# Mixer of a two-half megakernel: products of two units in one run of TensorE, four decay buffers, near decays by absolute value

## What is computed

```
xn    = layer norm of x (as the program fuses it), then per token:
proj  = xn @ in_proj_w.T          # gate 4096, x 4096, B 8*128, C 8*128, dt 64
xBC   = silu(causal conv of 4 taps over x, B, C)
dt    = softplus(dt + dt_bias);  dA = exp(-dt * exp(A_log))
state = state * dA + (dt * x) (outer) B         # for each of 64 heads, along the sequence
y     = state . C + D * x
y     = group rms norm(y) * norm_weight * silu(gate)
s     = y @ out_proj_w.T
out   : four-stream mixing of xn with 50 Sinkhorn iterations, a branch product, SiLU, times s, plus x
```

## Time and profile before

| | us |
|---|---|
| median of 3 runs (lowest, highest) | 3055.89 (3054.63, 3057.09) |
| the profiled execution, its own time | 3054.47 |
| its span | 3053.0 |
| TensorE busy | 3000.2 (98%) |
| weight loads busy | 2341.8 (77%) |
| VectorE busy | 2128.1 (70%) |
| ScalarE busy | 1763.6 (58%) |
| GpSimd busy | 687.7 (23%) |

### The profile page before, as it was taken

How to read it: one execution, slowest core, us unless ns; L and a number is a source line. 1 busy time by engine, 2 the same in 40 slices (tenths; PEclk the granted TensorE clock), 3 DMA queues, 4 the chain that set the end, 5 groups by cost and what they waited for, 6 DMA issues and landing times.

```text
span 3053.0 us, 45217 instructions
## 1 busy us (share of the span) xinstructions
PE 3000.2 (98%) x14352; PEld 2341.8 (77%) x14352; DVE 2128.1 (70%) x2648; ACT 1763.6 (58%) x3728; POOL 687.7 (23%) x575
## 2 busy tenths in 40 slices
PE   8999999999999998999999999999999999999998
PEld 7777777777777777777777777777777788887787
DVE  7667667576666685767666666766667878677877
ACT  5667575757666575576665757575665332234443
POOL 4222213121222134413222231212124000001112
PEclk9999999999999999999999999999999999999999
DMA  3534343443434353435243433434254444456665
GB/s 138 169 126 158 108 159 107 141 138 110 155 110 155 114 197 98 157 121 172 95 168 104 157 123 135 139 109 160 90 171 153 148 138 150 146 196 211 209 212 182
DMA packets 125532, 444.90 MB, mean 146 GB/s; under 512 B 17488, under 2 KB 21712, under 8 KB 109008
## 3 DMA queue, kind: packets, MB, share of 16 engines
q1 hardware_dynamic: 117552, 423.14, 41.1%
q0 software_dynamic: 4096, 14.68, 1.2%
q10 hardware_dynamic: 3744, 5.51, 0.6%
HBM read 397.86 MB, written 45.42 MB: 145 GB/s over the span
## 4 chain that ended last, share of the span: by engine, by line
PE 82%; issue 5%; DVE 4%; POOL 2%; ACT 2%; DMA 2%; DVEq 0%; SPq 0%; ACTq 0%; POOLq 0%
PE bank L1101 18%; PE bank L1103 17%; PE bank L1102 17%; PE bank L1139 9%; PE bank L1361 5%; PE bank L1362 5%; PE bank L1363 5%; PE bank L1113 2%; PE bank L1125 2%; DMA acc<-in_w_out 1%; PE bank L1149 1%; POOL gate L467 1%; DVE acc L839 1%; DVE x_lo L1356 1%; DVE x_lo L1355 1%
## 5 line engine op out<-in xcount | busy, mean ns | idle before, releaser
L1101 PE MATMUL bank<-x_hi,w_hi 128*128 128x512 f32 x2576 | 1024.6, 398 | 2.4 <-DVE acc L839 2.4
L1103 PE MATMUL bank<-x_hi,w_lo 128*128 128x512 f32 x2576 | 1003.0, 389 | 0.0
L1102 PE MATMUL bank<-x_lo,w_hi 128*128 128x512 f32 x2576 | 1000.9, 389 | 0.0
L839 DVE SCALAR_TENSOR_TENSOR acc<-bank,conv_w,acc 128x511 f32<-128x511 f32 (+2 forms) x576 | 430.8, 748 | 270.5 <-ACT acc L616 241.9
L1101 PEld LDWEIGHTS bank<-x_hi,w_hi 128*128 128x128 f32 x2576 | 484.1, 188 | 114.7 <-issue 22.2
L1103 PEld LDWEIGHTS bank<-x_hi,w_lo 128*128 128x128 f32 x2576 | 484.0, 188 | 102.6
L1102 PEld LDWEIGHTS bank<-x_lo,w_hi 128*128 128x128 f32 x2576 | 484.9, 188 | 93.6
L616 ACT ACTIVATE acc<-bank,tap_par 128x512 f32<-128x512 f32 x192 | 149.5, 779 | 517.0 <-PE bank L1103 486.0
L1361 PE MATMUL bank<-x_hi 128*128 128x512 f32 x1008 | 394.7, 392 | 8.9 <-DVE x_lo L1356 5.3
L1362 PE MATMUL bank<-x_lo,x_hi 128*128 128x512 f32 x1008 | 393.1, 390 | 0.0
L1363 PE MATMUL bank<-x_hi,x_lo 128*128 128x512 f32 x1008 | 392.9, 390 | 0.0
(11 more groups left out here) (165 smaller groups left out, 3408.0 us busy)
## 6 DMA issues: line engine op xcount, KB each, us to landing
units<-cum_scratch SPq DMA_DIRECT2D x128, 1280.0 KB, 6.7
w_raw<-in_w_in SPq DMA_DIRECT2D x160, 512.0 KB, 3.7
w_raw<-y_scratch SPq DMA_DIRECT2D x128, 512.0 KB, 3.6
y_scratch<-gate SPq DMA_DIRECT2D x32, 1024.0 KB, 6.5
acc<-in_w_out SPq DMA_DIRECT2D x128, 256.0 KB, 3.8
xbc<-in_x SPq DMA_DIRECT2D x16, 512.0 KB, 5.6
units<-in_x SPq DMA_DIRECT2D x16, 512.0 KB, 3.7
rstd_b<-rc_scratch SPq DMA_DIRECT2D x32, 256.0 KB, 4.3
```

The costliest lines, as they stand in the source:

```text
L839: dve.scalar_tensor_tensor(acc[:, s % 2, back:], bank_proj[s % 2][:, 0:SEQ - back], mix.conv_w[:, at, m, 3 - back:4 - back], acc[:, s % 2, ...
L1101: pe.matmul(out, w_hi[m % 2][:, k, :], hi, start=(k == 0), stop=False)
L1102: pe.matmul(out, w_hi[m % 2][:, k, :], lo, start=False, stop=False)
L1103: mm = pe.matmul(out, w_lo[m % 2][:, k, :], hi, start=False, stop=(k == KT - 1))
```

## The change

It has six parts. (1) `RING` 3 to 4: a fourth decay buffer. (2) The plans: products of two units stand in one slot, turns too, with slots for exponentials, weighing and turns written out; `turn_x` uses two banks, 2 and 7 (7 is also a bank of the scores), sums, `rc`, `rb`, `scale` and stores of both sequences move. (3) To make room in memory: `w_raw` and `th` with one buffer instead of two, the mask with 256 columns instead of 512 (what lies beyond is copied, not multiplied), the output's raw tiles in `xbc`. (4) Near decays: Abs with the negated running sum `falls` as bias instead of Relu with `cum`; far exponentials with the same bias and scale -1 instead of `dec`, and rows of the table stored accordingly (`far` with six tables in three dependent steps). (5) At slot 12 the last tanh and SiLU stand first. (6) Order of the last pieces among the output's first products, slots of the output's first loads, `load_small` behind unit 6.

```diff
-RING = 3
+RING = 4
-        self.w_raw = sb("w_raw", [P, 2, KT, P])
+        self.w_raw = sb("w_raw", [P, KT, P])
-        self.acc, self.th = sb("acc", [P, 2, SEQ]), sb("th", [P, 2, SEQ])
+        self.acc, self.th = sb("acc", [P, 2, SEQ]), sb("th", [P, SEQ])
-        self.cum = sb("cum", [P, NT, HEADS])
-        self.dec = sb("dec", [P, NT, HEADS])
+        self.falls = sb("falls", [P, NT, HEADS])
...
-        self.exp = exp or [s - 3 + h for s in mult for h in range(2)]
-        self.turn = [s - 2 for s in mult]
-        self.attn = [s - 1 for s in mult]
+        self.load, self.exp, self.attn, self.turn, self.mult = load, exp, attn, turn, mult
         self.square = [s + 1 for s in mult]
         self.gate = [max(s + 1, gate_from + 1 + u) for u, s in enumerate(mult)]
-        self.norm = [s + 2 for s in mult[-SEQS:]]
-        self.var = [s + 3 for s in mult[-SEQS:]]
-        self.rc = [s + 4 for s in mult[-SEQS:]]
-        self.rb = [s + 5 for s in mult[-SEQS:]]
-        self.scale = [s + 6 for s in mult[-SEQS:]]
-        self.store = [s + 7 for s in mult[-SEQS:]]
+        self.norm = [s + norm_after for s in mult[-SEQS:]]
+        self.var = [s + 1 for s in self.norm]
+        self.rc = [s + 3 for s in self.norm]
+        self.rb = [s + 3 for s in self.norm]
+        self.scale = [s + 4 for s in self.norm]
+        self.store = [s + 5 + q for q, s in enumerate(self.norm)]
...
-FIRST = Plan(cb=[9, 11], load=[9, 10, 12, 14, 15, 17, 19, 20], mult=[13, 14, 16, 18, 19, 21, 23, 24],
-LATER = Plan(cb=[5, 7], load=[4, 5, 7, 10, 12, 14, 16, 18], mult=[9, 11, 13, 15, 17, 19, 21, 23],
-LAST = Plan(cb=[5, 7], load=[4, 5, 7, 10, 12, 14, 15, 17], mult=[9, 11, 13, 14, 16, 18, 20, 21],
-            gate_from=CONV_SLOTS, exp=[6, 7, 8, 9, 10, 11, 11, 12, 13, 14, 15, 16, 17, 18, 18, 19])
+FIRST = Plan(cb=[9, 11], load=[9, 10, 12, 13, 16, 17, 19, 20],
+             exp=[10, 11, 12, 13, 13, 14, 15, 16, 17, 17, 18, 18, 20, 20, 21, 21],
+             attn=[12, 14, 16, 17, 19, 20, 22, 23], turn=[13, 13, 15, 15, 18, 18, 20, 20],
+             mult=[15, 15, 18, 18, 20, 20, 23, 23], gate_from=CONV_SLOTS, norm_after=3)
+LATER = Plan(cb=[4, 6], load=[5, 6, 9, 10, 13, 14, 17, 18],
+             exp=[6, 7, 8, 9, 10, 11, 12, 13, 14, 15, 16, 17, 18, 19, 20, 21],
+             attn=[8, 10, 12, 14, 16, 18, 20, 22], turn=[8, 8, 11, 11, 15, 15, 19, 19],
+             mult=[11, 11, 15, 15, 19, 19, 23, 23], gate_from=CONV_SLOTS, norm_after=3)
+LAST = Plan(cb=[4, 6], load=[5, 6, 8, 9, 12, 13, 15, 16],
+            exp=[6, 7, 8, 9, 9, 10, 11, 12, 13, 13, 14, 15, 16, 16, 17, 18],
+            attn=[8, 10, 11, 13, 15, 16, 18, 19], turn=[8, 8, 11, 11, 14, 14, 17, 17],
+            mult=[11, 11, 14, 14, 17, 17, 20, 20], gate_from=CONV_SLOTS, norm_after=2)
+OUTPUT_LOADS = [SLOTS - 5, SLOTS - 4]
...
-    bank_tr = core.bank[2]
+    bank_tr = [core.bank[2], core.bank[7]]
...
         def load_w(g, at, m):
             n = TILES * g + m
-            need(sp, w_split, n - 1)
-            sp.dma_start(w_raw[:, m % 2, :, :], w_tiles[TILES * at + ORDER[m]]).then_inc(w_loaded[m % 2], 16)
+            need(sp, w_split, n)
+            sp.dma_start(w_raw[:, :, :], w_tiles[TILES * at + ORDER[m]]).then_inc(w_loaded, 16)
...
-            need(sp, multiplied, UNITS * (half * GROUPS - 1) + UNITS - 2)
+            need(sp, multiplied, UNITS * (half * GROUPS - 1) + UNITS - 1)
             sp.dma_start(small_raw, d["w_small"]).then_inc(early_of[half].small_loaded, 16)
...
-                    ahead = s // 2 + 3
+                    ahead = s // 2 + 2
...
         def tanh(g, s):
             act.wait_ge(conv_taken, CONV_SLOTS * g + s + 1)
-            act.activation(th[:, s % 2, :], acc[:, s % 2, :], ACT.Tanh).then_inc(tanh_done, 1)
+            if s:
+                act.wait_ge(silu_done, CONV_SLOTS * g + s)
+            else:
+                need(act, gate_done, GATE_SLOTS * g)
+            act.activation(th[:, :], acc[:, s % 2, :], ACT.Tanh).then_inc(tanh_done, 1)
...
-                op = act.activation(part, part, ACT.Relu, bias=mix.cum[:, CHUNKS * q + k, head], scale=-1.0)
+                op = act.activation(part, part, ACT.Abs, bias=mix.falls[:, CHUNKS * q + k, head], scale=-1.0)
...
-                act.activation(part, part, ACT.Exp, bias=mix.dec[:, CHUNKS * q + k, head])
+                act.activation(part, part, ACT.Exp, bias=mix.falls[:, CHUNKS * q + k, head], scale=-1.0)
...
-                op = dve.tensor_tensor(bc[:, q, OFFSET[k]:OFFSET[k] + WIDTH[k]], cb_out[k],
-                                       core.mask[:, 0:WIDTH[k]], ALU.mult)
+                near = min(WIDTH[k], 2 * P)
+                if WIDTH[k] > near:
+                    dve.tensor_copy(bc[:, q, OFFSET[k] + near:OFFSET[k] + WIDTH[k]], cb_out[k][:, near:])
+                op = dve.tensor_tensor(bc[:, q, OFFSET[k]:OFFSET[k] + near], cb_out[k][:, 0:near],
+                                       core.mask[:, 0:near], ALU.mult)
...
             c, q = divmod(u, SEQS)
             pe.wait_ge(silu_done, CONV_SLOTS * g + 2 * SEQS + u + 1)
-            need(pe, dtx_done, UNITS * g + u)
+            need(pe, dtx_done, UNITS * g + u - 1)
+            if u == 1:
+                pe.wait_ge(bc_done, SEQS * (g + 1))
...
-        drain(piece, HALVES - 1, SLOTS, LAST.mult[-1])
+        pe.wait_ge(dtx_done, UNITS * HALVES * GROUPS)
         pe.wait_ge(bc_done, SEQS * HALVES * GROUPS)
         pe.wait_ge(gate_taken, GATE_SLOTS * HALVES * GROUPS)
         first_products(0, (3, 4, 7, 0, 1))
-        drain(piece, HALVES - 1, LAST.mult[-1], LAST.norm[0])
+        drain(piece, HALVES - 1, SLOTS, LAST.norm[0])
         first_products(1, (3, 4, 7, 0, 1))
-        drain(piece, HALVES - 1, LAST.norm[0], LAST.norm[1])
         pe.wait_ge(y_done, UNITS * HALVES * GROUPS)
         for j in range(2):
             first_products(j, (5, 6))
-        drain(piece, HALVES - 1, LAST.norm[1])
+        drain(piece, HALVES - 1, LAST.norm[0])
```

More of the change, by code:

```diff
@@ L175 @@
 SCALE_AT = [{t: [0, 1] if t == 0 else [t + 1] for t in range(NT - 1)}, {2: [4], 3: [5], 4: [6], 6: [7]}]
-RSTD_AT = [{t: [t] for t in range(NT)}, {1: [4], 3: [5], 4: [6], 6: [7]}]
+RSTD_AT = [{t: [t] for t in range(NT)}, {1: [4], 2: [5, 6], 5: [7]}]
 AHEAD_LOAD = [8, 8, 12, 15, 19]
@@ L255, in mixer_programs @@
     w_branch = sq[:, :].rearrange("p (k c) -> p k c", c=CW)
-    far = sums[:, 0, 0:3 * SEQS * HEADS].rearrange("p (a q h) -> p a q h", a=3, q=SEQS)
-    cum_hm = bc[0:HEADS, :, :]
-    causal, ones, one = core.mask[:, 0:P], core.mask[:, P:2 * P], core.mask[:, SEQ - 1:SEQ]
+    far = flat(sums)[:, 0:6 * SEQS * HEADS].rearrange("p (q a h) -> p q a h", a=6, q=SEQS)
+    rows_hm = bc[0:HEADS, :, :]
+    causal, ones, one = core.mask[:, 0:P], core.mask[:, P:2 * P], core.mask[:, 2 * P - 1:2 * P]
     d_heads = rstd_b[:, 1, 0:HEADS]
@@ L402, in step @@
                         load_w(g + 1, after(at, plan), ahead - TILES)
-                    elif ahead < TILES + 2:
-                        sp.wait_ge(w_split, TILES * g + ahead - 1)
-                        sp.wait_ge(silu_done, CONV_SLOTS * (g + 1))
-                        output.load(sp, 0, 0, ahead - TILES)
+                if ends_all(half, plan) and s in OUTPUT_LOADS:
+                    sp.wait_ge(cb_done, SEQS * (g + 1))
+                    sp.wait_ge(silu_done, CONV_SLOTS * (g + 1))
+                    output.load(sp, 0, 0, OUTPUT_LOADS.index(s))
                 for group in open_groups(g, s, half, plan, before):
@@ L1034, in early @@
                 dve.wait_ge(e.cum_copied, 1)
-                dve.tensor_tensor(far[:, 0], cum[:, :, 2, :], tot[:, :, 1, :], ALU.add).then_inc(e.far_step, 1)
-                dve.tensor_tensor(far[:, 1], cum[:, :, 3, :], tot[:, :, 2, :], ALU.add).then_inc(e.far_step, 1)
-                dve.wait_ge(e.far_step, 2)
-                dve.tensor_tensor(far[:, 2], far[:, 1], tot[:, :, 1, :], ALU.add).then_inc(e.far_step, 1)
-                dve.tensor_tensor(mix.dec[:, :, :], by_head(bank_tot[:, :]), mix.cum[:, :, :],
-                                  ALU.subtract).then_inc(e.far_step, 1)
+                for n in range(3):
+                    at = (0, 3, 5)[n]
+                    last = falls[:, :, 1:, :] if n == 0 else far[:, :, at - 3 + n:at, :]
+                    if n:
+                        dve.wait_ge(e.far_step, n)
+                    dve.tensor_tensor(far[:, :, at:at + 3 - n, :], last, tot[:, :, 0:3 - n, :],
+                                      ALU.subtract).then_inc(e.far_step, 1)
             t = s - 2
@@ L1248, in turn_cum @@
             need(pe, e.cum_hm_copied, 3 * q)
-            near = [mix.cum[:, CHUNKS * q + k, :] for k in range(CHUNKS)]
-            ahead = [far[:, a, q, :] for a in range(3)]
-            for i, table in enumerate([near[0], near[1], ahead[0], ahead[2], near[1], near[2], ahead[1],
-                                       near[2], near[3], near[3]]):
+            near = [mix.falls[:, CHUNKS * q + k, :] for k in range(CHUNKS)]
```

(3 more changed lines are left out.)

60 lines of the change are left out of this document (29 added, 31 removed).

## The result

The changed kernel takes 3084.79 us, the median of 5 runs (3082.01 to 3087.98), against 3056.06 of 5 runs of the kernel before: a ratio of 1.0092, 95% interval 1.0081 to 1.0103. It is slower by 28.7; 3061 was forecast, at most 3076.

The account below looks back on a forecast made before the run. TensorE was taken to set the time. Inner groups -15.6, FIRST +22.4, LAST -1.0, between halves -4.3 and end +3.3 sum to +4.8: 3059.3 for the profiled execution, 3061 as median; range 3040 to 3076.

Parts of the forecast that it names:

- Inner groups, -1.3 each: Six inner groups a half: fewer runs, shape changes and turns save 1.9, two returning waits leave -1.3 each, -15.6 for twelve.
- The wait of turn 1: Inner groups: turn 1 shares bank 7 with the scores and waits for both masks, 0.3.
- that of `project(10)`: Inner groups: `project(10)` waits for its bank until VectorE's conv, behind `split_lo` and `weigh`, is done, 0.3.
- FIRST, +11.2 for the group: FIRST, one group a half: six fewer runs -1.5, but late ScalarE and VectorE work makes products wait; +11.2 (8 to 15) each.
- 1.0 for the clock: FIRST: TensorE, idle while waiting, loses its clock and runs at 1.2 GHz instead of 2.4; 1.0 (0 to 3).
- LAST, -0.5 each: LAST groups, one a half: turns merged and one run fewer, -0.5 each, -1.0 in all.
- the cover of the single `w_raw`: Load goes out two slots ahead (11 us, needs 4); costed at nothing; if cover goes, each late microsecond is paid per tile.
- Between the halves, -4.3: From turn 7 to the transposes behind the second small product: 30.0 before, now shorter by 4.3 (-6 to -1).
- End of the mixer, +3.3: Last gate frees bank 1 late, so output products start later: +2.6 and 0.7 for the clock, +3.3 (0 to 5).
- The late store of the gate (b): Slower rival: second half of `gate` stored in slot 12 lands late, 14 groups pay 1.1: +15, 3076; chance 0.14.
- That of the clock (c): Slower rival: waits in FIRST and at the end leave 1.2 GHz stretches, 1.7 each: +6, 3066; part of a 0.2 chance.
- FIRST without its waits (a): Faster rival: ScalarE not so late in slot 1 behind FIRST; FIRST gives -1, total -19.6, 3036; chance 0.27.

Follow-up runs that it names:

- four small moves: Changed kernel, pairs kept: FIRST's squares 4, 5 and last head to slot 22; LAST's unit 4 load to slot 11, squares 4, 5 to 19: 3060.22, single execution.
- the run with the moved issue: Changed kernel with the load of unit 4's decays in slot 12 of LAST issued ahead of load_w instead of behind it: 3083.31, single execution.

## Why the prediction was wrong

**Inner groups, -1.3 each: right.** Ten of them gained 1.5 each (137.8 to 138.3 for the forecast 138.2). The wait of turn 1 did not come, that of `project(10)` did (0.2 in its row), and in some groups 0.2 before a gate.

**FIRST, +11.2 for the group, 9.9 with the inner group's own gain taken off: right in size.** Measured +10.5 and +11.4. Product 6 waits 6.3 where 6.2 stood in the sum, product 5 waits 2.6 where 1.3 stood, product 7 only 1.0 where 3.7 stood: while TensorE is late for product 6, VectorE goes on with the next conv and weighing. The half speed behind the wait took up the difference: from product 6 to product 7 it took 5.56, of which 1.03 waited, so product 6 itself took 2.2 more than the 2.30 of a plain one, where I had 1.0 for the clock. The weighing of unit 6 ended 22.9 behind the run in slot 20, for 22.7 in the sum. The microsecond lost to GpSimd fell on it (3.88), and only 0.3 on the low part, where I had put all of it.

**LAST, -0.5 each: this is the step that failed.** It stood in one sentence: "Turns merged, one run fewer". I had worked FIRST through from engine to engine and costed the other packed plan by TensorE's stream alone, as if ScalarE and VectorE were as far ahead as in LATER. Measured +11.9 and +6.9 up to slot 19, which is 19.8 of the 28.7 by which the sum fell short of the profiled execution. What the runs show in its place: with the slots of before the loss is gone (e.g. 170.46 for 170.44), four slots in place of three for units 2 and 3 take it away up to slot 19, the statistics make 5.3 of it in half 0, and the load behind `load_w` makes 4 in half 0; these overlap and do not add up. What was wrong is the overlap: ScalarE and VectorE were taken to be ready in LAST, and they are not with two units in three slots. I had even written that the cover of the single `w_raw` might go and what each late microsecond would then cost, and had looked for it behind FIRST alone.

**Between the halves, -4.3: measured -1.4.** From the end of slot 19 (1173.88) to the transposes behind the second small product (1202.33) it takes 28.5, where 25.7 was forecast. The order was right. The clock was not:

```profile
1162.00:1200.00 38.00, 31.17 (x165) 25.20 (x166) 24.90 (x37) 22.49 (x41) 24.64 (x27) 0.82 0.25 80
```

In 38 us 0.82 is granted. The first small product takes 5.03 where the second takes 2.88, and the products of each set of sums lie 1.51 apart from first to last instead of 0.70. I had 0.7 for it. Over the stage itself, 1173.9 to 1202.4, 0.76 is granted; before, from 1158.0 to 1188.1, it was 0.89.

**End of the mixer, +3.3: measured +8.8 to the end of the program, of which 1.1 lies behind the output's 91st product.** TensorE waits 6.6 where 5 was forecast, which is ScalarE's squares: the second starts 4.2 behind the first, not 2.73, because GpSimd's add between them took 2.90 instead of 1.3. The rest is the clock again (15 output products in 6.3 instead of 3.5) and a low part 1.7 late behind it.

**The rivals.** The late store of the gate (b) did not hold TensorE: no inner group is over 138.3. Its wait does exist in LAST. ScalarE stands 2.2 before the gate of slot 13 in half 0 and 3.6 in half 1, until 1126.87 and 2301.53; the stores issued at 1119.83 and 2293.15 had landed 7.0 and 8.3 later, 0.1 before. In both halves the decays came later still, so it cost nothing of its own. That of the clock (c) gave the right direction and less than it cost. FIRST without its waits (a) was wrong. None of them had the packing of LAST in it, so the range could not hold the result, 3084.8.

## What to carry to other kernels

A schedule written by hand has as many budgets as plans. Where an edit packs the same work into fewer slots, every engine's load per slot must be added up in every plan, and most carefully in the shortest one; the gain of the long plan says nothing of it. Here the pairs are worth 15 us where they have four slots each. Where two units had three slots or fewer the new plans cost 48, and the run with pairs in LATER only gets that back; with four small moves about half of it comes back although the pairs stay (3060.22).

Taking one wait away from a chain in which two engines are full moves the wait to the next link: three of the single moves ended in another wait. A cheap test is to give one stage its old plan back, and to read the stage and not the sum.

A buffer saved makes the wait on its load longer, and in a queue that issues in the program's order everything behind that load waits too, also what has nothing to do with the buffer.

## What the runs showed of the hardware

**A wait costs more than its length.** Behind the waits of 4.3 and over the products ran slow: the stretches behind two of them in LAST (the first rows are the wait, the second what followed):

```profile
1136.30:1141.50 5.20, 0.17 (x1) 0.00 (x0) 1.21 (x2) 5.20 (x14) 0.00 (x0) 0.71 0.01 4
1141.50:1147.50 6.00, 5.93 (x18) 4.80 (x19) 5.97 (x10) 6.00 (x18) 1.34 (x1) 0.68 0.83 256
...
2309.80:2314.40 4.60, 0.34 (x2) 0.00 (x0) 1.23 (x2) 4.60 (x13) 0.00 (x0) 0.81 0.00 0
2314.40:2328.00 13.60, 13.54 (x50) 11.02 (x51) 8.72 (x9) 12.13 (x30) 4.38 (x3) 0.81 0.89 332
```

The two slots at 2314.45 took 13.37 instead of 11.0, so 2.4 on top of a wait of 4.3; those at 1141.57 12.78, 1.8 on top of 5.1; the output products 2.7 on top of 6.6. The waits of 2.1 and 1.5 before slots 13 and 14 were followed by 24 products at the plain pitch. Between these the length alone does not decide: a wait of 2.6 (187.12 above) was followed by a product at the plain length of 2.38, one of 2.4 in the run with the moved issue by a product of 4.07. The Trainium skill ("TensorE: Matmul & The Clock Gate", section "What's actually happening") calls the throttled clock the default, released by activity. These rows agree in kind: behind the waits the products first start 0.43 apart and then 0.23, so the 0.68 and 0.81 are mixtures of half speed (1.2 GHz) and full speed (2.4 GHz). I had put at most 1.7 on such a wait.

**GpSimd and VectorE hold each other up both ways.** The timelines of VectorE and GpSimd at the end of the mixer:

```profile
2344.93 2.83 DVE L887 TENSOR_TENSOR units<-units,bc 128x2560 f32<-128x2560 f32 x1 [1.15 <-ACT units L665]
```
```profile
2345.98 2.90 POOL L478 TENSOR_TENSOR sums<-sums,sq 128x512 f32<-128x512 f32 x1 [13.69 <-ACT sq L678]
2350.12 1.27 POOL L478 TENSOR_TENSOR sums<-sums,sq 128x512 f32<-128x512 f32 x1 [1.24 <-ACT sq L678]
```

The add that started under a weighing ends 1.1 after it and took 2.90; the next, alone, took 1.27. With a weighing of 3.93 beside GpSimd the loss is on VectorE's side. The Trainium skill ("SBUF — State Buffer", section "Who interferes with whom" and the rules at its end) has the second to issue blocked until the first ends, where VectorE reads two inputs from SBUF and GpSimd reads it too. The add agrees: the weighing ends at 2347.76, an add of 1.27 from there ends at 2349.03, and it ended at 2348.88. The weighing of 3.93 lies under a run of GpSimd's products, and the rows do not show which of the two was first. I had used the rule for VectorE alone.

**A load flew longest where it was issued in a burst.** The tile view of `cum_scratch` (us from issue to landing: least, median, most), 1090 to 1145 in the changed kernel, and 1085 to 1145 in the kernel before:

```profile
DMA to landing us min/median/max: 7.1/10.1/15.0
```
```profile
DMA to landing us min/median/max: 6.3/7.2/9.7
```

A queue that stood for 13 us let go of five transfers within 3.0. The two decay loads among them, issued at 1120.31 and 1122.49, flew 12.9 and 15.0 (the same view, one issue at a time). The two outside the burst, issued at 1096.53 and 1141.91, flew 7.3 and 7.1.
